# Five raw weight buffers and written-out turns in a Perceiver kernel's expert stage

## What is computed

```python
x = x + cross_attention(ctx, layernorm(x))   # 16 heads of 64; 4096 context rows and the 256 latents as keys
x = x + performer(layernorm(x))              # linear attention: 16 heads of 16, 44 random features a head
x = x + moe(layernorm(x))                    # 8 experts, two a row, and a shared one: 9 pairs W1 [256, 1024], W2 [1024, 256]

def moe(x):
    probs = softmax(x @ Wg); vals, idx = top_k(probs, 2)
    share = scatter(idx, vals / sum(vals))
    y = sum(share[:, e] * (silu(x @ W1[e] + b1[e]) @ W2[e] + b2[e]) for e in range(8))
    return y + 0.1 * (silu(x @ Ws1 + bs1) @ Ws2 + bs2)
```

## Time and profile before

| what | value |
|---|---|
| median of three runs | 649.87 us |
| lowest and highest | 649.75 and 650.17 us |
| the profiled execution, its own time | 650.91 us |
| its span, first to last instruction | 649.2 us |
| granted TensorE clock over the span, 1 is 2.4 GHz | 0.997 |
| busy: PE, weight load, DVE, ACT, POOL | 638.5, 519.4, 501.9, 432.3, 243.6 us |
| attention, performer, experts (TensorE's part) | to 505.5, to 538.4, to 646.5 us |

### The profile page before, as it was taken

The page is one execution under the profiler, slowest core; times in us unless marked ns, Lnnn a source line. Parts: engine busy times, 40 slices in busy tenths (PEclk is TensorE's granted clock), DMA queues, the critical chain, the costliest instruction groups (busy, mean ns, idle before and its releaser), DMA issues.

```text
span 649.2 us, 14641 instructions
## 1 busy us (share of the span) xinstructions
PE 638.5 (98%) x5180; PEld 519.4 (80%) x5180; DVE 501.9 (77%) x1013; ACT 432.3 (67%) x931; POOL 243.6 (38%) x209
## 2 busy tenths in 40 slices
PE   8999999999999999999999999999999999999998
PEld 7777777777777777777777777777777878999998
DVE  5799999877887777678967776688676787977574
ACT  5788888877756776766766676776665434746561
POOL 3565556534332233332234323233320300563640
PEclk9899999999999999999999999999999999999999
DMA  7111450010000010000000000000000301765500
GB/s 214 60 48 34 128 155 2 17 34 2 1 2 18 2 50 2 3 1 2 2 17 2 2 2 1 2 2 6 14 2 1 131 1 67 249 206 194 187 7 17
DMA packets 26166, 30.53 MB, mean 47 GB/s; under 512 B 4201, under 2 KB 23794, under 8 KB 26098
## 3 DMA queue, kind: packets, MB, share of 16 engines
q1 hardware_dynamic: 24594, 28.86, 13.9%
q10 hardware_dynamic: 1504, 0.79, 0.4%
HBM read 29.38 MB, written 0.26 MB: 46 GB/s over the span
## 4 chain that ended last, share of the span: by engine, by line
PE 93%; DVE 3%; POOL 1%; issue 1%; ACT 1%; DMA 1%; DVEq 0%; POOLq 0%; ACTq 0%
PE kv_ps L172 29%; PE o_ps L527 19%; PE s_ps L514 16%; PE e_h_ps L172 8%; PE e_y_ps L1704 7%; PE s_ps L494 4%; PE o_ps L172 1%; PE s_ps L462 1%; PE o_ps L547 1%; PE f_ps L172 1%; PE f_ps L1329 1%; DMA x_res<-in_x 1%; DVE f_inverse L1543 1%; PE e_y_ps L1719 0%; PE e_bias_ps L1719 0%
## 5 line engine op out<-in xcount | busy, mean ns | idle before, releaser
L1145 POOL TENSOR_TENSOR k_rms<-k_ss,neg_half 128x4 f32<-128x4 f32 x136 | 162.7, 1198 | 265.0 <-DVE k_ss L952 265.0
L172 PE MATMUL kv_ps<-w_quad,xn 128*128 128x512 f32 x816 | 209.6, 405 | 1.0 <-DVE xn L895 0.6
L172 PEld LDWEIGHTS kv_ps<-w_quad,xn 128*128 128x128 f32 x816 | 148.9, 189 | 38.3 <-ACT z L708 0.8
L735 ACT ACTIVATE probs<-s_ps,minus_bound 128x512 f32<-128x512 f32 x204 | 124.0, 689 | 59.7 <-PE s_ps L514 59.6
L946 DVE SCALAR_TENSOR_TENSOR probs_sum<-probs,tile_mask,probs_sum 128x512 f32<-128x512 f32 x198 | 139.7, 746 | 28.2 <-ACT probs L735 28.2
L514 PEld LDWEIGHTS s_ps<-q_parts,kt 64*128 64x128 f32 x1632 | 100.9, 185 | 25.9 <-issue 25.1
L514 PE MATMUL s_ps<-q_parts,kt 64*128 64x256 f32 x1632 | 115.0, 286 | 0.0
L952 DVE TENSOR_REDUCE k_ss<-k_sq 128x4 f32<-128x256 f32 x136 | 56.5, 416 | 28.5 <-ACT k_sq L702 28.3
L527 PE MATMUL o_ps<-probs,v 128*64 128x256 f32 x544 | 64.7, 384 | 0.0
L946 DVE SCALAR_TENSOR_TENSOR probs_sum<-rows,tile_mask,probs_sum 128x512 f32<-128x512 f32 x66 | 45.9, 747 | 17.3 <-ACT rows L735 17.2
L735 ACT ACTIVATE rows<-s_ps,minus_bound 128x512 f32<-128x512 f32 x68 | 41.2, 689 | 25.1 <-PE s_ps L514 25.1
(11 more groups left out here) (247 smaller groups left out, 872.5 us busy)
## 6 DMA issues: line engine op xcount, KB each, us to landing
w_raw<-in_ffn_W SPq DMA_DIRECT2D x18, 1024.0 KB, 5.4
rows<-in_ctx SPq DMA_DIRECT2D x7, 512.0 KB, 3.9
w_raw<-in_L_xattn_Wkv SPq DMA_DIRECT2D x6, 256.0 KB, 3.6
wout<-in_L_xattn_Wout SPq DMA_DIRECT2D x4, 256.0 KB, 2.7
wq_raw<-in_L_xattn_Wq SPq DMA_DIRECT2D x3, 256.0 KB, 2.9
rows<-in_ctx SPq DMA_DIRECT2D x2, 256.0 KB, 5.2
w_raw<-in_L_xattn_Wkv ACTq DMA_DIRECT2D x2, 256.0 KB, 5.1
wq_raw<-in_L_xattn_Wq ACTq DMA_DIRECT2D x1, 256.0 KB, 3.9
```

The source lines that it names most:

```text
L172: last = nc.tensor.matmul(out, stationary(k, s), moving(k, m), start=n == 0, stop=n == len(terms) - 1)
L735: nc.scalar.activation(probs_at(n)[:, :, c, :], s_ps[n % 2][c][:], ACT.Exp, bias=minus_bound[:]).then_inc(exp_done, 1)
L1145: nc.gpsimd.tensor_tensor(k_rms[n % 2][:].rearrange("p i c -> p (i c)"), k_ss[n % 2][:].rearrange("p i c -> p (i c)"), neg_half[:, 0:4], A ...
```

## The change

1. `RAW = 5` raw buffers for W1 and for W2. Behind `attended`, SP loads Wg and b2 (before: behind `performed`) and then experts 1 to 4, eight transfers of 1 MB one behind the other. Experts 5 to 8 follow, each waiting for the low parts of expert n - 5.
2. In `experts` the loops on the engines are gone; every turn is written out on every engine, with constant waits and addresses.
3. Tiles are placed anew: the memset before `attended` writes `unread`, and the tile `ended` (4 bytes in a slot of 32) is gone, so that the attention's tiles behind it lie 32 bytes lower; in the performer and the experts the large tiles are allocated ahead of the small ones, so that they lie above the five raw buffers. `e_act_p`, for one, moves from byte 151776 of a partition to 190784, and `e_w2_second` from 116000 to 166208.
4. At the start of the attention TensorE gets 6 more unread matmuls between `project(1)` and `transpose_q(0)`, DVE does `scale_k(0)` ahead of `mean_square(1)` and `scale_k(1)` ahead of `offset(2)` and `center(2)`, and POOL does `root_of(2)` behind `root(0)` and `root(1)`.
5. Two more unread matmuls stand at the performer's start (7 for 5) and one more at the experts' (8 for 7).

```diff
+RAW = 5
...
     def rest(self, stay):
-        self.w1_raw.append(stay("w1_raw1", [P, KD, F]))
-        self.w2_raw.append(stay("w2_raw1", [P, FT, D]))
+        for b in range(1, RAW):
+            self.w1_raw.append(stay(f"w1_raw{b}", [P, KD, F]))
+            self.w2_raw.append(stay(f"w2_raw{b}", [P, FT, D]))
...
-        unread, ended = ring(1, "unread", [P, 1])[0], ring(1, "ended", [P, 1])[0]
+        unread = ring(1, "unread", [P, 1])[0]
...
             project(1)
+            keep_busy(nc, s_ps[1][1][:, 0, 0:P], ident[:], ident[:], 6)
             transpose_q(0)
...
             scale_q(0)
+            scale_k(0)
             mean_square(1)
             link(nc.vector.scalar_tensor_tensor(bound[:, 0:DH], gqk[:], -1.0, gqk[:], ALU.mult, ALU.max))
-            scale_k(0)
             link(nc.vector.reduce_max(bound[:, DH:DH + 1], bound[:, 0:DH], AX_X))
+            scale_k(1)
             offset(2)
             center(2)
-            scale_k(1)
...
             root_q(0)
-            root_of(2)
             root(0)
             root(1)
+            root_of(2)
             root(2)
...
             sp.wait_ge(attended, 1)
-            sp.dma_start(ew.w1_raw[1][:], a["ffn_W1"][1]...)
-            sp.dma_start(ew.w2_raw[1][:], a["ffn_W2"][1]...)
+            sp.dma_start(ew.wg[:], a["L0_ffn_Wg"]...)
+            sp.dma_start(ew.b2[:], a["ffn_b2"])
+            for n in range(1, RAW):
+                sp.dma_start(ew.w1_raw[n][:], a["ffn_W1"][n]...)
+                sp.dma_start(ew.w2_raw[n][:], a["ffn_W2"][n]...)
...
-            busy(0, 5)
+            busy(0, 7)
...
-            run(sp, load, 2, E1, 2)
+            for n in range(RAW, E1):
+                sp.wait_ge(w1_lo, n - RAW + 1)
+                sp.dma_start(w1_raw[n % RAW][:], a["ffn_W1"][n]...)
+                sp.wait_ge(w2_lo, n - RAW + 1)
+                sp.dma_start(w2_raw[n % RAW][:], a["ffn_W2"][n]...)
...
-            keep_busy(nc, h_ps[:, 4, :], ident[:], fw.w["Wq"][:, 0, :], 7)
+            keep_busy(nc, h_ps[:, 4, :], ident[:], fw.w["Wq"][:, 0, :], 8)
...
-            run(pe, turn, 2, E1, 2)
+            for n in range(2, E1):
+                turn(Turn(n, 2))
```

More of the change, by code:

```diff
@@ L118, in __init__ @@
         self.b1 = keep("b1", [P, E + 1, FT])
-        self.w1_in, self.w2_in = [sem(f"w1_in{b}") for b in range(2)], [sem(f"w2_in{b}") for b in range(2)]
+        self.w1_in, self.w2_in = [sem(f"w1_in{b}") for b in range(RAW)], [sem(f"w2_in{b}") for b in range(RAW)]
+        self.b2_in, self.wg_in = sem("b2_in"), sem("wg_in")
         self.b1_in, self.numbered = sem("b1_in"), sem("numbered")
@@ L128, in rest @@
         self.w1_second = stay("w1_second", [P, KD, 2, F], F32R)
+        self.b2, self.wg = stay("b2", [E + 1, D]), stay("wg", [P, KD, E])
         self.number = stay("number", [P, E], mybir.dt.int32)
@@ L990, in add_heads @@
                 dve.wait_ge(y_added, added)
-                nc.vector.memset(ended[:], 0.0).then_inc(attended, 1)
+                nc.vector.memset(unread[:], 0.0).then_inc(attended, 1)
             statistics(0)
@@ L1659, in _ @@
             pool.wait_ge(act_lo, 4)
-            run(pool, lo1, 3, E1, 2)
+            for n in range(3, E1):
+                lo1(Turn(n, 2))
         @block.tensor
         def _(pe):
-            keep_busy(nc, h_ps[:, 4, :], ident[:], fw.w["Wq"][:, 0, :], 7)
+            keep_busy(nc, h_ps[:, 4, :], ident[:], fw.w["Wq"][:, 0, :], 8)
             pe.wait_ge(z_done, 1)
@@ L1787, in _ @@
             hi2(Turn(1, 2))
-            run(act, turn, 1, E1 - 1, 2)
+            for n in range(1, E1 - 1):
+                turn(Turn(n, 2))
             silu(Turn(E1 - 1, 2))
@@ L1877, in _ @@
             lo2(Turn(2, 2))
-            run(dve, turn, 2, E1 - 1, 2)
+            for n in range(2, E1 - 1):
+                turn(Turn(n, 2))
             split_act(Turn(E1 - 1, 2))
```

60 lines of the change are left out of this document (28 added, 32 removed).

## The result

| | before | changed |
|---|---|---|
| median (extremes), us | 650.34 (649.75 to 651.69), 20 runs | 651.47 (650.68 to 653.97), 20 runs |
| profiled execution, us | 650.91 | 651.8 |
| its span, us | 649.2 | 650.1 |
| ratio, 95% interval | | 1.0017 (1.001 to 1.0023) |

The change costs 0.17%: too little to be told from no change by the bound of 0.2%, and 3 us from the forecast's 648.4, outside its range. Two things happened inside: the attention became shorter by more than anybody asked for, and the performer and the experts gave it back and more.

The account below looks back on a forecast made before the run. TensorE was taken as the bound, busy 638.5 of 649.2 us. From 650.91, 0.7 (start) and 0.8 (loops) gave 649.4 profiled; less 1.04 for the profiled execution's distance from the median, 648.4 us, range 646.6 to 650.8.

Parts of the forecast that it names:

- Part 2: Experts' turns without loops: slow `up` turns 2 to 4 become 5.45 us, 0.8 us less in sum, bounds 0 and 2.7.
- Part 3: Attention's start reordered: low clock at 19 to 23 us avoided, 0.7 us gained, bounds 1.7 gained and 1.0 lost.
- Part 1: Expert weights loaded from about 507 us, landed by 532: term 0, as TensorE had not waited for them.
- Part 5: Tiles' new places, attention's moved by 32 bytes: term 0, since no row says place sets a matmul's pace.
- 7 us either way: End of the tile-places term: 3.7% of the kv matmuls' 188 us, not taken into the range.
- the slow spacing has another cause and stays: Lower bound of the no-loops term in the experts' turns: gain 0.
- performer and experts' opening as long as before: Sign expected in the new profile: the stretch from 505.5 to 544.2 us stays at 38.7 us.
- every step of it: Attention's start: kv's second pair (`project(2)`) at 17.5, scores at 22.3, TensorE's wait for `xn` of unit 3 at 32.8 us.
- Part 4: Three more unread matmuls at performer's and experts' start: term 0, upper end 0.2 us each, hidden inside existing waits.
- Slower, by the places: Rival, chance 0.10: kv matmuls slowed by `w_quad` moving 32 bytes, up to +7 us; from +2.8 it leaves 651.2.

Follow-up runs that it names:

- experiments 1 and 2: 1: tile `ended` removed (32-byte shift) in the kernel before, 648.98 us, ratio 0.9967; 2: `ended` put back in the changed kernel, 653.98 us, ratio 1.0049.
- experiments 6 and 7: 6: kernel before, only `zp` moved by 832 bytes, 652.14 us; 7: changed kernel, experts' tiles back at their old places modulo 1024 bytes, 649.5 us.
- experiment 5: Kernel before with the experts' turns written out on every engine and nothing else: 650.44 us, ratio 1.0005.
- experiment 3: Changed kernel with the weights of experts 2 to 4 loaded after the performer: 650.17 us, ratio 0.9996.
- experiment 8: Kernel before with the four edits of the attention's start alone: 650.55 us, ratio 1.0002.
- experiment 12: Kernel before with unused bytes alone, placed to give the best operand differences for kv, `up` and `down`: 646.99 us, ratio 0.9946.
- experiment 10: Kernel before with the 32-byte shift, the start's four edits and the three more unread matmuls: 648.74 us, ratio 0.9968.
- experiment 11: Separate kernel without the computation, only timing fp32r matmuls in `up` and kv forms at varied tile offsets: `up` form 119.6 ns at difference 0, 113.3 at 192.
- experiments 4 and 7: Changed kernel; 4: 192 unused bytes ahead of `zp` alone, 651.25 us; 7: all experts' tiles back at their old places modulo 1024 bytes, 649.5 us.

## Why the prediction was wrong, point by point

The forecast was a gain of 1.5 us, 0.8 from the turns and 0.7 from the start, and the kernel lost 1.1 (1.4 at full clock). Three steps made that error: the gain of Part 2 was not there (0.8), the gain of Part 3 was not there and 0.2 to 0.3 came on top (0.9 to 1.0), and the loads of Part 1 cost 1.3 to 1.6 where 0 stood. The largest error of mechanism, Part 5, does not show in the total at all, since its two halves of 2.2 us cancel: that is luck. The forecast's base, three runs of before at 649.87, was another 0.5 below the 20 runs of the result.

- **Part 5, the places**, had the mechanism wrong. It said "Term 0", "I do not take such an end into the range", and reached 0 by the argument that no row says that place is the condition. It was two terms: -2.25 us in the attention (experiments 1 and 2) and +2.2 us in the turns (experiments 6 and 7). The two paces of `up` in the earlier trace rows, from which it took its bound, are those of one and the same set of places, so they were no measure of what a new place does; their cause is the one that stays open. A bound was known (7 us either way) and left out of the range, without a row that ruled it out. The 16-byte lines of the Trainium skill (Advanced Engine Details and Errata, "SBUF Cachelines") led the prediction to the same 0, as a shift of 32 bytes keeps every place within its line. The measurement decides: 2.25 us, and a period of 256 bytes.
- **Part 2, no loops**, said that the three slow `up` turns are slow because they are the first in the loop (-0.8). Written out in the kernel before, three turns were slow all the same (experiment 5, 102.23 for 102.24 us). The slow turns only moved from 2 to 4 to 0 to 2. The term measured 0.0 where 0.8 was forecast; its lower bound, "the slow spacing has another cause and stays", was right.
- **Part 1, the loads**, said 0, and "performer and experts' opening as long as before". The wait that it had wrong is DVE's and TensorE's for POOL's reduction: +1.6 us in the trace, -1.3 us in the median when taken out (experiment 3). The argument looked at who waits for the weights, and never at who works while they move: POOL's reduction had 5.6 us of "issue" ahead of it and then more. By the statement of the Trainium skill that transfers and engines cannot contend (SBUF — State Buffer, "SBUF: two separate sides") nothing would have been held up in SBUF; this instruction started 3.5 us later beside the transfers, and whether the hold-up is in SBUF at all no run shows. The weights landed by 532, as said.
- **Part 3, the start**: every step of it was seen (17.66, 22.68, 32.88), and the gain forecast at 0.7 us was not one. The working compared with the profiled execution, which had its low clock at the start and was 1.04 us above the median of three. The prediction had that number, and subtracted it at the end as if it were noise. It was the time of the low clock (1.2 us between the medians), which most executions do not have, so taking 0.7 for avoiding it and 1.04 on top counted it twice. At full clock the reordered start is 0.2 us slower in the median and 0.3 in the profiles (experiment 8), as `z` comes later and TensorE waits 0.88 us for it.
- **Part 4** was right: the three more unread matmuls show nowhere; with the loads out of the performer its stretch is 37.13 us as before.
- **The rival "Slower, by the places"** had the mechanism, in the wrong matmuls and, for kv, with the wrong sign. That kv gained what the turns lost is chance of the layout, and that the total came out by its 651.2 is chance too.

The sum with what was measured at full clock: -2.25 (shift), +1.6 (loads), +2.2 (experts' places), +0.2 (start), 0 (loops, unread matmuls) is +1.75 by profiles; the medians at full clock say 651.4 - 650.0 = +1.4. With the 1.3 us that the loads are worth in the median the sum is 1.45.

Open stays: what chooses between two paces at the same difference (three turns, five or all nine slow, and `down` in experiment 12); what holds the reduction up while weights load; and what brings the low clock. Before it came there were 1.0 and 1.2 us of idle TensorE in one case (the start of before); in experiment 10, where it came at 501.6 us, TensorE had been busy for 19.94 of the 20 us from 480 to 500.

## What to carry to other kernels

Where TensorE is busy all the time, the tiles' addresses are a cost of their own: here up to 3% (512 columns) and 5% (256) of a fp32r matmul's time, by moving start minus stationary start modulo 256 bytes. So any edit that adds, drops or moves a tile should be read with the addresses of both builds beside it, and timed against a variant that pads them back: 32 bytes were worth 2.25 us here and 800 bytes of padding 3.6, where the whole change cost 1.4. And when the profiled execution lies a microsecond from the median, find out which row holds that microsecond before a gain is counted on it.

## What had not been expected of the hardware

- fp32r matmuls of 128x128 by 256 columns took 113.7 to 119.7 ns and by 512 columns 227.2 to 234.5 ns with all other engines idle, by the difference of the two operands' places alone (experiment 11); fp32 ones of 128x64 did not vary (104.6).
- At one and the same difference two paces are to be had, 113.3 and 117.8 ns (118.7 and 120.0 in experiment 6), each for a whole turn of 48 matmuls or several. Which one it is may hang on tiles that these matmuls do not read (experiments 4 and 7).
- POOL's reduction over partitions started 8.0 to 9.0 us after the instruction ahead of it with 8 MB loading, and 5.5 to 5.7 us without.
- The low clock came in 24 of 70 executions of an unchanged kernel, and cost 1.2 us between the medians. In each of the six profiles that show it, it came once, for 3.4 us, at one of three places (from 18.5 or 19.5, from 501.6 or 504.1, from 531.6 or 531.9 us). Four executions of other kernels had more of it (means of 0.995, 0.995, 0.990 and 0.987).
